# A transformer block on one core: attention with plain float32 products, scores in 32-row groups, value bias folded into the output bias

## The reference, cut to what is computed

```python
def _L0_attn_ref(x, Wq, bq, Wk, bk, Wv, bv, Wo, bo):
    B, S, DIM, H = (2, 1024, 512, 16)      # x is (8, 1024, 512); 16 heads of 32
    q = _split_heads(x @ Wq.T + bq)
    k = _split_heads(x @ Wk.T + bk)
    v = _split_heads(x @ Wv.T + bv)
    q = jnp.exp(q)
    k = jnp.exp(k)
    kv = jnp.cumsum(k[:, :, :, None] * v[:, :, None, :], axis=1)
    k1 = jnp.cumsum(k, axis=1)
    num = jnp.einsum('zsD,zsDd->zsd', q, kv)
    den = jnp.sum(q * k1, axis=-1, keepdims=True)
    out = num / den
    return out @ Wo.T + bo                 # heads merged

x = L0_attn_x
x = x + 0.5 * _L0_ffn_ref(_layernorm(x, axis=-1), gate_w, gate_b, w1, w2)
x = x + _L0_attn_ref(_layernorm(x, axis=-1), Wq, bq, Wk, bk, Wv, bv, Wo, bo)
x = x + 0.5 * _L0_ffn_ref(_layernorm(x, axis=-1), gate_w, gate_b, w1, w2)
```

## Time and profile before

| | us |
|---|---|
| three runs | 2999.12, 2992.57, 2998.35 |
| median | 2998.35 |
| the profiled execution, its time | 2993.34 |
| its span (first to last instruction) | 2991.6 |
| TensorE busy / weight loads busy | 2459.0 / 1436.8 |
| VectorE, ScalarE, GpSimd busy | 1303.4, 669.0, 328.2 |
| first experts end, attention's first matmul | 783.9, 796.1 |
| last chunk of attention starts (its residual, line 906) | 2207.3 |

### The profile page before, as it was taken

One profiled execution on the slowest core, in us unless ns is written; L12 is line 12 of the kernel. 1 busy time (PEld: TensorE's weight loads), 2 busy tenths in 40 slices (PEclk: granted clock), 3 DMA queues, 4 the chain that ended last, 5 costly groups with the idle time before them and its releaser, 6 DMA issues.

```text
span 2991.6 us, 35578 instructions
## 1 busy us (share of the span) xinstructions
PE 2459.0 (82%) x14836; PEld 1436.8 (48%) x14836; DVE 1303.4 (44%) x2320; ACT 669.0 (22%) x1167; POOL 328.2 (11%) x344
## 2 busy tenths in 40 slices
PE   7866666666599999999999999999996666666668
PEld 4321211111277777777777777777773111111113
DVE  8600000000276777777777777776772000000006
ACT  7500000000132333333333333333331000000000
POOL 2100000000021121221112112112210000000000
PEclk9998988999899999999999999999997988989989
DMA  5699999999500000000000000000008999999999
GB/s 193 251 382 424 425 423 425 424 424 425 228 22 22 29 22 22 29 22 22 22 29 22 22 28 23 22 22 29 22 15 326 424 425 425 424 424 425 425 409 351
DMA packets 106832, 637.82 MB, mean 213 GB/s; under 512 B 9360, under 2 KB 9360, under 8 KB 57520
## 3 DMA queue, kind: packets, MB, share of 16 engines
q1 hardware_dynamic: 99376, 621.91, 50.9%
q10 hardware_dynamic: 7296, 13.63, 1.2%
HBM read 597.75 MB, written 37.75 MB: 212 GB/s over the span
## 4 chain that ended last, share of the span: by engine, by line
PE 59%; DMA 37%; DVE 2%; ACT 1%; issue 1%; SPq 0%; POOL 0%; ACTq 0%; DVEq 0%; POOLq 0%
PE ps L260 54%; DMA big<-in_L_ffn_w 36%; PE ps L264 5%; DMA big<-in_L_attn_Wq 1%; DVE big L268 1%; DMA wtl<-wl_scratch 0%; PE ps L365 0%; DVE at L268 0%; PE ps L339 0%; ACT at L868 0%; DVE qb L268 0%; SPq L18 0%; DMA big<-in_L_attn_x 0%; DVE big L489 0%; ACT big L360 0%
## 5 line engine op out<-in xcount | busy, mean ns | idle before, releaser
L260 PE MATMUL ps<-big 128*32 128x512 f32 (+3 forms) x8512 | 1244.9, 539 | 461.2 <-DMA big<-in_L_ffn_w 394.4
L260 PEld LDWEIGHTS ps<-big 128*32 128x32 f32 (+1 forms) x8512 | 421.1, 123 | 1176.4 <-DMA big<-in_L_ffn_w 562.5
L618 DVE COPY big<-ps 128x512 f32<-128x512 f32 x64 | 44.3, 692 | 1068.5 <-PE ps L582 1068.5
L268 DVE TENSOR_TENSOR big<-ps,big 128x512 f32<-128x512 f32 (+1 forms) x584 | 384.0, 684 | 95.4 <-PE ps L260 93.0
L260 PE MATMUL ps<-wth,xth 128*128 128x512 f32 x768 | 313.3, 408 | 3.1 <-DVE xtl L268 3.1
L260 PE MATMUL ps<-wth,xtl 128*128 128x512 f32 x768 | 300.7, 392 | 0.0
L260 PE MATMUL ps<-wtl,xth 128*128 128x512 f32 x768 | 299.9, 391 | 0.0
L260 PE MATMUL ps<-qb,kt 128*128 128x512 f32 x768 | 196.1, 404 | 4.3 <-DVE qb L268 4.3
L260 PE MATMUL ps<-wth,at 128*128 128x512 f32 x512 | 176.2, 405 | 8.4 <-DVE at L268 8.4
L268 DVE TENSOR_TENSOR qb<-ps,qb 32x512 fp32r<-32x512 f32 x256 | 175.3, 685 | 6.5 <-ACT qb L845 0.5
L606 ACT ACTIVATE big<-ps 128x512 f32<-128x512 f32 x64 | 38.2, 597 | 617.8 <-PE ps L260 617.8
(11 more groups left out here) (83 smaller groups left out, 2036.9 us busy)
## 6 DMA issues: line engine op xcount, KB each, us to landing
big<-in_L_ffn_w SPq DMA_DIRECT2D x256, 2048.0 KB, 17.7
big<-in_L_attn_x SPq DMA_DIRECT2D x16, 1024.0 KB, 8.7
big<-in_L_attn_x SPq DMA_DIRECT2D x64, 256.0 KB, 2.8
x_scratch<-big SPq DMA_DIRECT2D x64, 256.0 KB, 2.0
out_x<-big SPq DMA_DIRECT2D x64, 256.0 KB, 4.8
big<-x_scratch SPq DMA_DIRECT2D x44, 256.0 KB, 7.6
big<-x_scratch ACTq DMA_DIRECT2D x20, 256.0 KB, 6.6
wl_scratch<-wls ACTq DMA_DIRECT2D x16, 256.0 KB, 7.7
```

Of the source, the lines that this page charges most:

```text
L260: return nc.tensor.matmul(o, l, r, start=start, stop=stop, skip_group_check=True)
L268: return nc.vector.tensor_tensor(o, p, q, op)
L618: nc.vector.tensor_copy(HT[i], ps[:, 2 + i, :]).then_inc(s_ht, 1)
```

## The change

All split products of attention become plain float32 products. The high and low halves (`WTH`/`WTL`, `XTH`/`XTL`, `KTH`/`KTL`, `QBH`/`QBL`, `ATH`/`ATL`, `KH`/`KL`) become one float32 tile each (`WT`, `XT`, `KT`, `QT`, `AT`, `Ks`), the instructions that made the low halves go, and so do the DRAM scratch, its 16 writes and its reading back. The scores are 16 matmuls of 32 rows by 128 columns: in group g, head r uses rows 32r to 32r + 31 of `KT` and `QT` and writes bank 4 + r. In the value stage the four products with the state stand ahead of the 16 by column groups. The value bias is not added to the values: since each row of weights sums to one, `Wo` times `bv` is added once to the output bias, by four matmuls and one VectorE addition ahead of the loop, and ScalarE copies the values out of PSUM in place of VectorE's addition. Banks and the order within a turn are new. Ring slots 0 and 1 are free in attention, so chunks 128 and 129 are loaded at n = 1, and chunk 130 takes slot 7.

```diff
-            return {4 * E: 0, 4 * E + 1: 7}.get(g, (g - 1) % 4)
+            return (0, 1, 7)[g - 4 * E] if g < 4 * E + 3 else (g - 1) % 4
...
-                nxt = g + 5 if g == 4 * E else None if g == 4 * E + 1 else g + 4
+                nxt = g + 5 if g < 4 * E + 2 else None if g == 4 * E + 2 else g + 4
...
+                nc.scalar.copy(WT[m][:, kt, :], ps[:, k, :]).then_inc(s_wt_, 1)
...
         def attention_sp(sp):
-            sp.wait_ge(d_wls[0], 16 * 8)
-            sp.wait_ge(d_wls[1], 16 * 8)
-            sp.wait_ge(s_used, 4 * E)
-            for m in range(4):
-                sp.dma_start(WTL[m].bitcast(F), wl[m].rearrange("k p n -> p k n")).then_inc(d_wl, 16)
-
...
+                if n == 1:
+                    load_chunk(sp, 128)
+                    load_chunk(sp, 129)
                 if n == NT - 2:
-                    sp.wait_ge(s_pk, NT)
-                    load_chunk(sp, 128)
                     sp.wait_ge(s_resid, NT)
-                    load_chunk(sp, 129)
+                    load_chunk(sp, 130)
...
-                    load_chunk(sp, 130)
                     load_biases(sp)
...
+        def project_pe(n, w, k):
             for j in range(4):
-                mm(ps[:, k, :], XTH[i][:, j, :], WTH[w][:, j, :], j == 0, False)
-                mm(ps[:, k, :], XTH[i][:, j, :], WTL[w][:, j, :], False, False)
-                t = mm(ps[:, k, :], XTL[i][:, j, :], WTH[w][:, j, :], False, j == 3)
+                t = mm(ps[:, k, :], XT[n % 2][:, j, :], WT[w][:, j, :], j == 0, j == 3)
...
-            pe.wait_ge(d_wl, 64)
-            pe.wait_ge(s_tri, 2)
+            pe.wait_ge(s_wt_, 16)
+            pe.wait_ge(d_bias, 16 * 7)
+            for g in range(4):
+                t = mm(ps[:, 1, :], BVT[:, g:g + 1].broadcast_to([128, 128]), WT[3][:, g, :], g == 0, g == 3)
+            t.then_inc(s_bo, 1)
+            pe.wait_ge(s_tri, 1)
             pe.wait_ge(s_o, 8)
+            pe.wait_ge(s_bo2, 1)
...
                     pe.wait_ge(s_pr, n + 1)
-                    mm(ps[:, 2, :], AFTER, KH, False, False)
-                    mm(ps[:, 2, :], AFTER, KL, False, False).then_inc(s_after, 1)
+                    mm(ps[:, 2, :], AFTER, Ks[i], False, False)
+                if live:
+                    pe.wait_ge(s_ke, n + 1)
+                    pe.wait_ge(s_xt3, n - 1)
+                    transpose4(4, Ks[i]).then_inc(s_ktT, 1)
+                    pe.wait_ge(s_qn, n + 1)
+                    pe.wait_ge(s_v, n + 1)
+                    transpose4(5, Qs[i]).then_inc(s_qtT, 1)
+                if nxt:
+                    pe.wait_ge(s_xt, n + 2)
+                    pe.wait_ge(s_L3, n - 1)
+                    project_pe(n + 1, 0, 0).then_inc(s_pq, 1)
+                if live:
+                    pe.wait_ge(s_kt, n + 1)
+                    pe.wait_ge(s_kvm, kvs(n))
+                    pe.wait_ge(s_qt, n + 1)
+                    for g in range(4):
+                        for r in range(4):
+                            R_ = slice(32 * r, 32 * r + 32)
+                            t = mm(ps[:, 4 + r, 128 * g:128 * g + 128], h4(KT)[R_, g, :], h4(QT)[R_, g, :], True, True)
+                            if g == 3:
+                                t.then_inc(s_S, 1)
+                if nxt:
+                    pe.wait_ge(s_x2, n)
+                    project_pe(n + 1, 1, 1).then_inc(s_pk, 1)
...
                     m = n + 2
-                    pe.wait_ge(s_xt3, n - 1)
-                    pe.wait_ge(s_x1, m)
+                    if nxt:
+                        pe.wait_ge(s_qb, n + 2)
                     mm(ps[:, 0, :], M[0][:, m // 32, 128 * (m % 8):128 * (m % 8) + 128], OBD[:, m // 8, :], True,
                        True).then_inc(s_resid, 1)
...
-                    pe.wait_ge(s_ktl, n + 1)
-                    pe.wait_ge(s_qbh, 4 * n + 4)
-                    pe.wait_ge(s_qbl, 4 * n + 4)
-                    for g in range(4):
-                        if nxt and g >= 2:
-                            pe.wait_ge((s_qb, s_kb)[g - 2], n + 2)
-                        mm(ps[:, 4 + g, :], h4(KTH)[:, g, :], QBH[:, g, :, :], True, False)
-                        mm(ps[:, 4 + g, :], h4(KTH)[:, g, :], QBL[:, g, :, :], False, False)
-                        mm(ps[:, 4 + g, :], h4(KTL)[:, g, :], QBH[:, g, :, :], False, True).then_inc(s_S, 1)
...
-                    project_pe(pe, n + 1, 2, 1).then_inc(s_pv, 1)
+                    if live:
+                        pe.wait_ge(s_st, 4 * n + 2)
+                    project_pe(n + 1, 2, 5).then_inc(s_pv, 1)
...
                     pe.wait_ge(s_st, 4 * n + 4)
+                    if c:
+                        for g in range(4):
+                            mm(ps[:, 3, 128 * g:128 * g + 128], h4(KV)[:, g, :], h4(QT)[:, g, :], g == 0, False)
                     for g in range(4):
-                        if c:
-                            mm(ps[:, 3, 128 * g:128 * g + 128], h4(KV)[:, g, :], h4(QT)[:, g, :], True, False)
                         for r in range(4):
                             o = ps[32 * r:32 * r + 32, 3, 128 * g:128 * g + 128]
                             t = mm(o, Vs[i][:, 128 * g + 32 * r:128 * g + 32 * r + 32],
-                                   ST[:, g, 128 * r:128 * r + 128], c == 0, True)
+                                   h4(ST[:, r, :])[:, g, :], c == 0, True)
                     t.then_inc(s_av, 1)
...
-                    pe.wait_ge(s_kl, n + 2)
+                    pe.wait_ge(s_ke, n + 2)
                     pe.wait_ge(s_pr, n + 1)
-                    mm(ps[:, 2, :], UPTO, KH, (n + 1) % 8 == 0, False)
-                    mm(ps[:, 2, :], UPTO, KL, False, False).then_inc(s_upto, 1)
+                    mm(ps[:, 2, :], TRI, Ks[(n + 1) % 2], (n + 1) % 8 == 0, False).then_inc(s_upto, 1)
...
+                if 0 <= n + 2 < NT:
+                    pe.wait_ge(s_xn, n + 3)
+                    pe.wait_ge(s_xt, n + 2)
+                    transpose4(7, XN).then_inc(s_xtT, 1)
...
-                    pe.wait_ge(s_atl, n + 1)
+                    pe.wait_ge(s_kb, min(n + 2, NT))
+                    pe.wait_ge(s_x2, n)
+                    pe.wait_ge(s_at, n + 1)
                     for g in range(4):
-                        mm(ps[:, 6, :], h4(ATH)[:, g, :], WTH[3][:, g, :], g == 0, False)
-                        mm(ps[:, 6, :], h4(ATH)[:, g, :], WTL[3][:, g, :], False, False)
-                        t = mm(ps[:, 6, :], h4(ATL)[:, g, :], WTH[3][:, g, :], False, g == 3)
+                        t = mm(ps[:, 1, :], h4(AT)[:, g, :], WT[3][:, g, :], g == 0, g == 3)
                     t.then_inc(s_op, 1)
...
+                    pe.wait_ge(s_x1, min(n + 3, NT))
...
-                    act.wait_ge(s_qb0, 2)
-                    for r in range(4):
-                        R_ = slice(32 * r, 32 * r + 32)
-                        nc.scalar.copy(QBH[R_, :, r, :], h4(ps[R_, 5, :])).then_inc(s_qbh, 1)
...
+                    act.wait_ge(s_pv, n + 2)
+                    act.wait_ge(s_av, n)
+                    act.wait_ge(s_kv, kvs(n))
+                    nc.scalar.copy(Vs[j], ps[:, 5, :]).then_inc(s_v, 1)
...
+            dve.wait_ge(d_bias, 16 * 7)
+            dve.wait_ge(s_bo, 1)
+            tt(BO, ps[:, 1, :], BO, ALU.add).then_inc(s_bo2, 1)
...
-            def split_q(n, r):
-                R_ = slice(32 * r, 32 * r + 32)
-                dve.wait_ge(s_qbh, 4 * n + r + 1)
-                tt(QBL[R_, :, r, :], h4(ps[R_, 5, :]), QBH[R_, :, r, :].bitcast(F), ALU.subtract).then_inc(s_qbl, 1)
...
+                    for r in range(4):
+                        dve.wait_ge(s_S, 4 * n + r + 1)
+                        tt(h4(ST[:, r, :]), h4(ps[:, 4 + r, :]), TRI.unsqueeze(1).broadcast_to([128, 4, 128]),
+                           ALU.mult).then_inc(s_st, 1)
...
-                if nxt:
-                    dve.wait_ge(s_pv, n + 2)
-                    dve.wait_ge(s_av, n)
-                    dve.wait_ge(s_kv, kvs(n))
-                    tt(Vs[j], ps[:, 1, :], BV, ALU.add).then_inc(s_vb, 1)
...
-                if live:
-                    dve.wait_ge(s_ath, n + 1)
-                    tt(ATL, ps[:, 3, :], ATH.bitcast(F), ALU.subtract).then_inc(s_atl, 1)
```

More of the change, by code:

```diff
@@ L22, in macaron_block @@
     F = mybir.dt.float32
-    R = mybir.dt.float32r
     ALU = mybir.AluOpType
@@ L31, in macaron_block @@
     EPS = 1e-5
-    wl = nc.dram_tensor("wl_scratch", (4, 4, 128, D), F).ap()
     x2d = nc.dram_tensor("x2_scratch", (B, S, D), F).ap()
@@ L75, in macaron_block @@
         GT = a.take(128).rearrange("p (k e) -> p k e", k=4)
-        BQ, BK, BV, BO = (a.take(512) for _ in range(4))
+        BQ, BK, BO = (a.take(512) for _ in range(3))
+        BVT = a.take(512)[:, 0:4]
         SM = a.take(256)
@@ L93, in macaron_block @@
         PR = TMP
-        kh_at = a.at
-        a.take(1024)
         ath_at = a.at
-        a.take(1024)
+        a.take(512)
         assert a.at <= SIZE
@@ L105, in macaron_block @@
         X2, XN = s.take(512), s.take(512)
```

(26 more changed lines are left out.)

201 lines of the change are left out of this document (53 added, 148 removed).

## The result

The changed kernel takes 3021.34 us (median of three runs, 3020.77 to 3021.42) against 2998.35: ratio 1.0082, 95% interval 1.0059 to 1.0105. The forecast was 3016. The profiled execution took 3021.42, its span is 3019.3; before they were 2993.34 and 2991.6, so there are 28.1 us to find.

A forecast was written before the change was run, and what follows sets the result against it. TensorE's instructions bound attention, DMA the experts. Attention +36, first experts -9.9, attention's start -5.2 and second experts -3 made +18 us on the profiled 2993.34, so 3011; 5.0 more to the median gave 3016, range 2996 to 3062.

The forecast's parts named there:

- bounds for the second: Scores in attention: 1.21 us a chunk if row groups overlap like column groups, 4.0 without overlap; 1.21 taken, -1.65.

The follow-up runs named there:

- run 1: The kernel before with only the value stage's four state products moved ahead of its 16 column-group matmuls: 2945.17 us, ratio 0.983.
- mix: The changed kernel with split float32r products again at full size and the value bias added in the loop by VectorE: 2823.67 us, ratio 0.9426.

## What to carry to other kernels

Where TensorE is the bound, price a change in TensorE's instructions alone, from start to start of a section, and price each part by itself: here the value stage in one block gains some 50 us (run 1), the scores in row groups with the new order some 120 (`mix` less run 1; the scores' section alone, 1.55 us a chunk, is 100 of them, and was not tried by itself), and the plain products lose 200. One trace of before gave the first and the last, and bounds for the second. A plain float32 product of 512 columns costs 0.857 us on this chip and three float32r ones 0.70, so split the large products and leave plain float32 to the small ones, in row or column groups that take turns.

## What the runs showed of the hardware

- The order in the queue decides how far row groups overlap: going round the four groups 1.31 us, one group after the other 2.97, for the same 32 instructions, and there each group starts halfway through the one before.
- A float32r matmul behind transposes shows its start 0.08 us early: a group of four transposes then reads 0.36 from start to start and the first matmul 0.31, where they take 0.44 and 0.23. Price such neighbours together.
- A block of row groups has 0.4 us of borders around 0.9 of work, one of column groups 0.3 around 0.9 (1.01 and 0.10 before, 0.10 behind).
